# Quarters of a projection between table matmuls, a cumulative sum in halves inside the tile loop, and a plan moved behind a low part

## The chip, the cores and the metric

The kernel runs on one core of a Trainium2 chip. The metric is the device time of one execution in microseconds (us). PE is TensorE, DVE is VectorE, ACT is ScalarE, POOL is GpSimd, SP is SyncE.

## The reference

The input x has 2 x 1024 tokens of 256 columns. It is normalised per row (xn). Two branches are added to x:

- **Attention branch (a minGRU in log space).** k = xn W_z^T + b_z and y = xn W_h^T + b_h. Then `log_coeffs = -softplus(k)`, `log_values = -softplus(-k) + g(y)`, where g is log(relu(y) + 0.5) for y >= 0 and -softplus(-y) otherwise. a_star is the cumulative sum of `log_coeffs` **over the 256 columns** of each token, padded by a zero row; `log_h = a_star + cumlogsumexp(log_values - a_star)` along the tokens, with an initial value from h0. log_h is normalised by its global mean and deviation, exponentiated, added to xn and normalised per row with a weight and a bias.
- **Expert branch.** A router takes the softmax of xn w_gate^T, the top 2 of 8 experts per token, with weights that sum to 1. Each expert computes silu(x w1^T) * (x w3^T), then w2^T, with 704 hidden columns, scaled by the token's weight and summed.

## The kernel before

All token data lie transposed (256 columns as two groups of 128 partitions, 2048 tokens along the row) in four chunks of 512 tokens, c = 0 to 3. U holds the growing log values, A the growing softplus sums. Chunks 0 and 1 are the first batch, 2 and 3 the second.

**Front.** PE transposes xn, computes router logits and the projections: `project(c, mat, parts)` (L1183) has four matmuls, mat 0 for k and mat 1 for y. ACT reads them (`k_part`, L511, two activations; `k_log`, L517, abs, exp, log; `h_part`, L524, four activations). DVE works out which token goes to which slot of which tile of 128 rows (each expert has whole tiles, some 35 tiles in all). Eight groups of one-hot matmuls (the tables, L1256 to L1263, m = 0 to 7) turn that into index tables; DVE makes the one-hot matrix of each group (L896) in one of two buffers, so it may not be more than two ahead. After the last group DVE reads the table (L902 to L910): the gather index lets POOL start the row gathers (`gather(j)`, L384, four ahead), which PE transposes (`x_tile`, L1265), ACT rounds to a high part (`x_hi`) and DVE completes with a low part (`x_lo`).

**Cumulative sum.** It runs over the columns, that is over partitions: a triangular matrix times A for the first group, ones plus triangle for the second. `cumsum(c)` (L1201) does both groups of a chunk, six instructions of 512 columns, into two PSUM banks; DVE adds the result to U and to A (`add_cumsum`, L948). `half_cumsum(c, q)` (L1211) does one group into one bank, `add_half` (L957) adds it. Before, chunks 0 and 1 use the whole form ahead of the tile loop, chunks 2 and 3 the half form in tiles 4 to 7.

**Tile loop.** Tile j: PE runs `up(j)` (18 instructions of two column parts and a rest, L1301), the transposes of x for tile j+1, hooks (`between(j)`), `down(j-1)` (L1319), then `h_tile(j)` (L1331), the transposes of the gated rows, which need DVE's `gate(j)` (L976), which needs ACT's `silu(j)` (L608). ACT copies hT as a high part (`h_hi`, L603, for tile 0 L625), DVE makes its low part (`h_lo`, L971). DVE's own hooks `between(j)` and `after(j)` hold the attention work: add_l3, less_n, less_l2, run_max and so on, each a step on 1024 columns of a chunk or a group.

**Weights.** The next expert's weights are split in four pieces into high (ACT, L617) and low (POOL, L425) parts while the current expert's tiles run. `tile_experts` (L857) and `tile_plan` (L880) on DVE compute from the routing how many pieces are due by each tile; ACT and POOL read `plan` and wait for it (s_ctl) before their first pieces. SP reloads a piece's raw buffer when POOL is done with it (L339).

The order of all this is written out by hand, per engine; nothing plans it.

Of the kernel before, what the change touches and what calls it, by code (L numbers as in the profile page):

```python
# [39 lines left out]
CH = 512  # L40
# [12 lines left out]
def build_program(nc, x, small, w_main, w_tail, out, xn_dram):  # L53
# [5 lines left out]
    with ctx:  # L59
# [14 lines left out]
        A = sb("A", [P, 2 * NTOK])  # L74
# [26 lines left out]
        where, start = {}, 0  # L101
# [375 lines left out]
        def _(act):  # L477
# [33 lines left out]
            def k_part(c):  # L511
                act.wait_ge(s_kp, c + 1)
                for q in range(Q):
                    act.activation(chunk_of(U, c)[:, q, :], k_ps[:, q * CH:(q + 1) * CH], ACT.Identity,
                                   bias=bias_sb[:, 0, q:q + 1]).then_inc(s_kb, 1)

            def k_log(c):  # L517
                l1 = chunk_of(A, c)
                act.wait_ge(s_kb, 2 * c + 2)
                chain(act.activation(l1, chunk_of(U, c), ACT.Abs))  # L520
                chain(act.activation(l1, l1, ACT.Exp, scale=-1.0))
                act.activation(l1, l1, ACT.Ln, bias=1.0).then_inc(s_l1, 1)

            def h_part(c):  # L524
                act.wait_ge(s_k, c + 1)
                for sign, dst, b in ((1.0, chunk_of(xnT_M, c), bias_sb[:, 1, :]), (-1.0, nns[c], nbias[:, :])):
                    for q in range(Q):
                        act.activation(dst[:, q, :], yh_ps[:, q * CH:(q + 1) * CH], ACT.Relu,  # L528
                                       scale=sign, bias=b[:, q:q + 1]).then_inc(s_yr, 1)
# [11 lines left out]
            def h_log1p(c):  # L541
                act.wait_ge(s_ex, c + 1)
                act.activation(l2s[c], l2s[c], ACT.Ln, bias=1.0).then_inc(s_l2, 1)
# [29 lines left out]
            def x_hi(j, slot, src=xT_ps):  # L573
                act.wait_ge(s_xt, j + 1)
                act.activation(xT[:, slot, 0, :].rearrange("p (q n) -> p q n", q=Q), src, ACT.Copy).then_inc(s_xhi, 1)  # L575
# [9 lines left out]
            for c in range(2):  # L585
                h_log(c)
                h_exp(c)
                h_log1p(c)
            k_log(2)
            k_part(3)  # L590
            k_log(3)
            x_hi(0, 0, xT0_ps)
            x_hi(1, 1, xT1_ps)
            act.wait_ge(s_idx, 1)
            row_weight(0)
            row_weight(1)
            h_part(3)
            act.preload_act_table_set("silu_and_others")

            def h_hi(j):  # L600
# [16 lines left out]
                        act.activation(wslot(p // PIECES + 1, 0, part), raw[:, ds(part, WP)], ACT.Copy).then_inc(s_hi, 1)  # L617
                return done

            act.wait_ge(s_uc[0], 2)  # L620
            act.wait_ge(s_uc[1], 1)
            silu(0)
            act.wait_ge(s_ctl, 1)
            act.wait_ge(s_ht, 1)
            act.activation(hT[:, 0, :], hT_ps, ACT.Copy).then_inc(s_hhi, 1)  # L625
            split_due(0, 0)

            def y_copy(j):
# [115 lines left out]
        def _(dve):  # L744
# [203 lines left out]
            def add_cumsum(c):  # L948
                dve.wait_ge(s_cum, c + 1)
                u_wait(c)  # L950
                u_step(c, dve.tensor_tensor(chunk_of(U, c), chunk_of(U, c), grid(cum_ps), ALU.add))
                ins = dve.tensor_tensor(chunk_of(A, c), chunk_of(A, c), grid(cum_ps), ALU.add)
                a_step(c, ins)
                dve.wait_ge(s_ac[c], 1)
                dve.sem_inc(s_E, 1)

            def add_half(c, q):  # L957
                n = 2 * (c - 2) + (1 - q)
                dve.wait_ge(s_cumh, n + 1)
                u_wait(c)  # L960
                u_step(c, dve.tensor_tensor(chunk_of(U, c)[:, q, :], chunk_of(U, c)[:, q, :], cumh_ps, ALU.add))
                a_step(c, dve.tensor_tensor(chunk_of(A, c)[:, q, :], chunk_of(A, c)[:, q, :], cumh_ps, ALU.add))
# [115 lines left out]
            softplus(0)  # L1078
            softplus(1)
            tile_experts()  # L1080
            add_cumsum(0)
            less_l2(0)
            less_l2(1)
            x_lo(0, 0, xT0_ps)
            softplus(2)
            add_cumsum(1)
            x_lo(1, 1, xT1_ps)
            dve.wait_ge(s_u0b, 2)
            step(dve.tensor_tensor(u0t[:, 5, :], u0t[:, 3, :], u0t[:, 4, :], ALU.subtract))
            for b in range(B):  # L1090
                step(dve.tensor_tensor(u0[:, :].rearrange("p (q b) -> p q b", b=B)[:, :, b], u0t[:, 5, :],
                                       u0t[:, 0, :], ALU.add))
            gate(0)
            tile_plan()
            h_lo(0)
            add_l3(0)
            softplus(3)

            def between(j):
                if j == 1:  # L1100
                    less_n(0)
                if j == 2:
                    less_n(2)
                if j in (4, 5, 6, 7):
                    add_half(j // 2, 1 - j % 2)
                if j == 3:
                    run_max(0)
                if j in (8, 9):
                    run_max(j - 6)
                if j in (10, 12):  # L1110
                    run_scan(j - 10)
                if 13 <= j <= 16:
                    plus_max(j - 13)
                if 20 <= j <= 27:
                    row_stats(j - 20)

            def after(j):
                if j == 1:
                    add_l3(1)
                    less_n(1)  # L1120
                if j == 2:
                    less_n(3)
                if j == 3:
                    max_steps(0)
                    less_max(0)
                if j == 4:
                    run_max(1)
                if j == 5:
                    max_steps(1)
                    less_max(1)  # L1130
                if j == 6:
                    add_l3(2)
                    add_l3(3)
                if j == 7:
                    less_l2(2)
                    less_l2(3)
                if j in (8, 9):
                    max_steps(j - 6)
                    less_max(j - 6)
                if j in (11, 12):  # L1140
                    run_scan(1 if j == 11 else 3)
                if 13 <= j <= 16:
                    logh(j - 13)
                    if j < 16:
                        log_stats(j - 13)
                    else:
                        sums()
                if j == 17:
                    squares()
                if j == 18:  # L1150
                    normaliser()
                if j in (24, 28):
                    row_scales((j - 24) // 4)
                if 24 <= j <= 31:
                    last_norm(j - 24)
# [20 lines left out]
        def _(pe):  # L1176
# [21 lines left out]
                if n == 3:  # L1198
                    ins.then_inc(s_k if mat else s_kp, 1)

            def cumsum(c):  # L1201

                pe.wait_ge(s_c, c + 1)
                if c:
                    pe.wait_ge(s_E, c)
                pe.matmul(cum_ps[:, 0:CH], tri[:, :], chunk_of(A, c)[:, 0, :], start=True, stop=True)
                pe.matmul(cum_ps[:, CH:2 * CH], ones[:, :], chunk_of(A, c)[:, 0, :], start=True, stop=False)
                pe.matmul(cum_ps[:, CH:2 * CH], tri[:, :], chunk_of(A, c)[:, 1, :], start=False,
                          stop=True).then_inc(s_cum, 1)

            def half_cumsum(c, q):  # L1211

                n = 2 * (c - 2) + (1 - q)
                pe.wait_ge(s_c, c + 1)
                if n:
                    pe.wait_ge(s_ac[(n - 1) // 2 + 2], (n - 1) % 2 + 1)
                if q:
                    pe.matmul(cumh_ps, ones[:, :], chunk_of(A, c)[:, 0, :], start=True, stop=False)
                pe.matmul(cumh_ps, tri[:, :], chunk_of(A, c)[:, q, :], start=(q == 0), stop=True).then_inc(s_cumh, 1)
# [38 lines left out]
            for m in range(2 * NT // 4):  # L1258
                pe.wait_ge(s_pos, m + 1)
                for s in range(4):  # L1260
                    r = 4 * m + s
                    ins = pe.matmul(table_ps, onehot_pos[:, m % 2, s * P:(s + 1) * P],
                                    onehot_tile[:, r * NCOL:(r + 1) * NCOL], start=(r == 0), stop=(r == 2 * NT - 1))  # L1263
                ins.then_inc(s_posu, 1)

            def x_tile(j, k, val, dst=xT_ps):

# [1 line left out]
                for q in range(Q):  # L1269
                    ins = pe.transpose(dst[:, q, :], xg[:, k, q * P:(q + 1) * P], ident[:, :])  # L1270
                ins.then_inc(s_xt, 1)
            project(3, 0)
            cumsum(0)
            project(3, 1)
            x_tile(0, 0, 16, xT0_ps)
            x_tile(1, 1, 16, xT1_ps)
            cumsum(1)

            def either(e, products):

# [52 lines left out]

            pe.wait_ge(s_kb, 2 * NCH)
            up(0, 0, 0, lambda: pe.wait_ge(s_yr, 4 * NCH))
            pe.wait_ge(s_E, 2)
            h_tile(0)
            pe.wait_ge(s_eid, 1)

# [20 lines left out]
                ins.then_inc(s_htr, 1)  # L1360

            def between(j):
                if j in (4, 5, 6, 7):
                    half_cumsum(j // 2, 1 - j % 2)
                if 20 <= j <= 27:
                    h_back(j - 20)
# [69 lines left out]
```

## Time and profile before

| | us |
|---|---|
| median of three runs | 352.63 (350.98 to 352.78) |
| the profiled execution | 352.66 |
| its span | 350.8 |
| PE busy | 323.4 (92%) |
| DVE busy | 243.4 (69%) |
| ACT busy | 229.2 (65%) |
| POOL busy | 204.4 (58%) |

The shares are means over the whole span. The stretch that the change touches lies between 42 and 110 us: the tables, the first tile, and tiles 1 to 4. A group of rows below is read as: start, duration, engine, line, operation, and in brackets how long the engine was idle before it and what ended that. "Issue" is time in which the engine waited for nothing that the profile shows.

### The profile page before, as it was taken

The page shows a single profiled execution, that of the slowest core. Times are in us where ns is not written, and L with a number is a line of the kernel's source. Part 1 is how long each engine was busy: PE and PEld are TensorE (multiplying, and loading weights), DVE is VectorE, ACT ScalarE, POOL GpSimd, SP SyncE. Part 2 cuts the span into 40 slices and gives each one's busy share as a digit, 9 for nine tenths or more (in the row PEclk, how much of TensorE's full clock was granted, in tenths as well). Part 3 has the DMA queues.
Part 4 walks back from the last instruction along what each step waited for, and adds up shares of the span by engine and source line. Part 5 has one row for each costly group of instructions (what it writes and reads, how often), then busy time and mean ns, then how long its engine had stood idle before and what let it go on. Part 6 is the DMA issues. An engine that isn't in the chain of part 4 may idle for free.

```text
span 350.8 us, 6683 instructions
## 1 busy us (share of the span) xinstructions
PE 323.4 (92%) x1964; PEld 272.7 (78%) x1964; DVE 243.4 (69%) x430; ACT 229.2 (65%) x365; POOL 204.4 (58%) x137
## 2 busy tenths in 40 slices
PE   8998999898999999899989899999999999999950
PEld 8773474587878889788878788789998997999940
DVE  5488778989996779959889942455498767553410
ACT  2548898564889993899974349963955565443420
POOL 4600004249977763897789927765398458863531
PEclk9999969999999999999999999999999999999995
DMA  7952922005434642345346432544265265456431
GB/s 258 347 215 94 308 87 60 17 0 160 101 98 92 167 97 48 76 101 141 58 87 164 98 56 41 142 105 101 33 157 139 61 77 92 50 90 84 56 49 15
DMA packets 19087, 37.01 MB, mean 105 GB/s; under 512 B 2272, under 2 KB 13536, under 8 KB 19008
## 3 DMA queue, kind: packets, MB, share of 16 engines
q0 software_dynamic: 9168, 11.97, 21.7%
q1 hardware_dynamic: 8496, 22.56, 20.7%
q10 hardware_dynamic: 1376, 1.85, 1.5%
q8 instruction: 29, 0.48, 0.6%
q14 instruction: 18, 0.15, 0.1%
HBM read 27.45 MB, written 11.03 MB: 110 GB/s over the span
## 4 chain that ended last, share of the span: by engine, by line
PE 28%; issue 17%; ACT 15%; DVE 15%; DMA 13%; POOL 6%; POOLq 2%; ACTq 2%; DVEq 0%
PE PS L1301 9%; DMA out<-work,sidx 7%; PE PS L1195 7%; DMA out<-xrow 5%; PE PS L1319 4%; ACT L718 3%; POOL work L390 2%; PE PS L1331 2%; POOL out L406 2%; DVE tmp L976 2%; ACT tmp L608 2%; ACT L710 2%; ACT wbuf L617 2%; DVE hT L971 2%; DVE A L1013 1%
## 5 line engine op out<-in xcount | busy, mean ns | idle before, releaser
L1301 PE MATMUL PS<-wbuf,xT 128*128 128x512 f32 (+1 forms) x648 | 148.0, 382 | 4.4 <-issue 3.5
L1301 PEld LDWEIGHTS PS<-wbuf,xT 128*128 128x128 f32 x648 | 117.2, 188 | 28.3 <-issue 8.7
L425 POOL TENSOR_TENSOR wbuf<-raw,wbuf x28 | 78.7, 2822 | 27.4 <-ACT wbuf L617 26.6
L406 POOL DMA_INDIRECT out<-work,sidx x35 | 62.2, 1778 | 46.9 <-ACT work L634 24.8
L1319 PE MATMUL PS<-wbuf,hT 128*128 128x256 f32 x648 | 86.8, 288 | 0.0
L1319 PEld LDWEIGHTS PS<-wbuf,hT 128*128 128x128 f32 x648 | 79.3, 189 | 1.9 <-issue 1.9
L390 POOL DMA_INDIRECT work<-xn_dram,gidx x39 | 51.2, 1312 | 50.2 <-DVE gidx L907 36.8
L971 DVE TENSOR_TENSOR hT<-PS,hT 128x768 fp32r<-128x768 f32 x36 | 34.2, 950 | 46.1 <-ACT hT L603 45.1
L608 ACT ACTIVATE tmp<-PS 128x512 f32<-128x512 f32 x72 | 31.6, 459 | 38.8 <-PE PS L1301 38.7
L976 DVE TENSOR_TENSOR tmp<-tmp,PS 128x512 f32<-128x512 f32 x72 | 34.9, 515 | 28.8 <-ACT tmp L608 27.9
L1331 PE MATMUL PS<-ident,tmp 128*128 128x128 f32 x216 | 30.2, 276 | 6.1 <-DVE tmp L976 6.0
L634 ACT ACTIVATE work<-PS,wrow 128x256 f32<-128x256 f32 x35 | 16.4, 469 | 29.3 <-PE PS L1319 29.3
L603 ACT ACTIVATE hT<-PS 128x768 fp32r<-128x768 f32 x35 | 28.3, 810 | 10.5 <-PE PS L1331 10.5
L617 ACT ACTIVATE wbuf<-raw x28 | 30.4, 1110 | 4.7 <-issue 4.6
L1195 PE MATMUL PS<-xnT_M,small_sb 128*128 128x512 f32 x64 | 31.0, 624 | 1.7 <-ACT tmp L528 1.0
L1331 PEld LDWEIGHTS PS<-ident,tmp 128*128 128x128 f32 x216 | 23.9, 141 | 8.7 <-DVE tmp L976 7.7
L1195 PEld LDWEIGHTS PS<-xnT_M,small_sb 128*128 128x128 f32 x64 | 12.1, 202 | 14.0 <-issue 12.8
L710 ACT ACT_TABLE_LOAD x14 | 18.0, 1283 | 0.3
L718 ACT ACT_TABLE_LOAD x14 | 18.0, 1283 | 0.2
L967 DVE TENSOR_TENSOR xT<-PS,xT 128x256 fp32r<-128x256 f32 x37 | 15.5, 418 | 0.1
L575 ACT ACTIVATE xT<-PS 128x256 fp32r<-128x256 f32 x37 | 14.0, 382 | 1.6 <-PE PS L1270 1.6
L581 ACT ACTIVATE wrow<-work,first_pick 128x1 f32<-128x1 f32 x37 | 14.1, 385 | 0.0
(186 smaller groups left out, 367.3 us busy)
## 6 DMA issues: line engine op xcount, KB each, us to landing
raw<-w_main SPq DMA_DIRECT2D x24, 544.0 KB, 4.0
raw<-w_main SPq DMA_DIRECT2D x8, 416.0 KB, 3.5
xn_dram<-xrow SPq DMA_DIRECT2D x4, 516.0 KB, 5.9
out<-xrow POOLq DMA_DIRECT2D x4, 512.0 KB, 6.5
xrow<-x ACTq DMA_DIRECT2D x4, 256.0 KB, 5.8
xrow<-x SPq DMA_DIRECT2D x4, 256.0 KB, 5.2
small_sb<-small ACTq DMA_DIRECT2D x1, 768.0 KB, 8.3
work<-xn_dram,gidx POOLq DMA_INDIRECT x39, 4.1
```

The costliest lines, as they stand in the source:

```text
L390: pool.indirect_dma_start(xg[:, k, :], None, xn_dram, bass.IndirectOffsetOnAxis(gidx[:, j:j + 1], 0)).then_inc(s_gt[k], 16)
L406: pool.indirect_dma_start(out, bass.IndirectOffsetOnAxis(sidx[:, j:j + 1], 0), ysb[:, j % DEEP, :], None, compute_op=ALU.add).then_inc(s_s ...
L425: pool.tensor_tensor(lo, raw[:, ds(part, WP)], hi.bitcast(fp32), ALU.subtract).then_inc(s_w, 1)
L608: act.activation(sls[n], w1_ps[n], ACT.Silu).then_inc(s_silu, 1)
L617: act.activation(wslot(p // PIECES + 1, 0, part), raw[:, ds(part, WP)], ACT.Copy).then_inc(s_hi, 1)
L718: act.preload_act_table_set("silu_and_others")
L971: dve.tensor_tensor(hT[:, 1, :], hT_ps, hT[:, 0, :].bitcast(fp32), ALU.subtract).then_inc(s_hlo, 1)
L976: dve.tensor_tensor(g_hs[n], sls[n], w3_ps[n], ALU.mult).then_inc(s_g, 1)
L1195: ins = pe.matmul(PS[:, base + qo * CH:base + (qo + 1) * CH], wzh_sb[:, q, mat, qo * P:(qo + 1) * P], xnT[:, q, c * CH:(c + 1) * CH], star ...
L1301: ins = pe.matmul(PS[:, at:at + cols], xT[:, slot, xpart, q * P:(q + 1) * P], wbuf[:, w, wpart, q * 2 * F + at:q * 2 * F + at + cols], sta ...
L1319: ins = pe.matmul(y_ps, hT[:, hpart, c * P:(c + 1) * P], wbuf[:, w, wpart, W13 + c * D:W13 + (c + 1) * D], start=(c == 0 and hpart == 0 an ...
L1331: ins = pe.transpose(hT_ps[:, c * P:(c + 1) * P], g_h[:, a:a + P], ident[:, :])
```

## The change

PE: the four matmuls of `project(3, 0)` stand one each behind the table groups m = 3, 4, 5, 6, instead of all four behind the last group. `cumsum` is left for chunk 0 only, behind `project(3, 1)`. Chunk 1's sum becomes two half sums in the PE hook of tiles 1 and 2, and the waits of the half form count from chunk 1.

ACT: `k_part(3)` ahead of `k_log(2)`, `h_part(3)` ahead of the two x_hi, `k_log(3)` behind them. The wait for the plan moves behind the copy of hT in tile 0.

DVE: less_l2 and both x_lo ahead of `add_cumsum(0)`; `add_cumsum(1)` goes, `add_half(1, 1)` and `add_half(1, 0)` come into the hooks of tiles 1 and 2; `h_lo(0)` ahead of `tile_plan()`; add_l3 and less_n of chunks 0 to 3 change places within tiles 0 to 2.

```diff
@@ ACT @@
+            k_part(3)
             k_log(2)
-            k_part(3)
-            k_log(3)
+            h_part(3)
             x_hi(0, 0, xT0_ps)
             x_hi(1, 1, xT1_ps)
+            k_log(3)
             act.wait_ge(s_idx, 1)
             row_weight(0)
             row_weight(1)
-            h_part(3)
...
-            act.wait_ge(s_uc[0], 2)
+            act.wait_ge(s_uc[0], 1)
             act.wait_ge(s_uc[1], 1)
             silu(0)
-            act.wait_ge(s_ctl, 1)
             act.wait_ge(s_ht, 1)
             act.activation(hT[:, 0, :], hT_ps, ACT.Copy).then_inc(s_hhi, 1)
+            act.wait_ge(s_ctl, 1)
             split_due(0, 0)
@@ DVE @@
             tile_experts()
-            add_cumsum(0)
             less_l2(0)
             less_l2(1)
             x_lo(0, 0, xT0_ps)
+            x_lo(1, 1, xT1_ps)
+            add_cumsum(0)
             softplus(2)
-            add_cumsum(1)
-            x_lo(1, 1, xT1_ps)
...
             gate(0)
+            h_lo(0)
             tile_plan()
-            h_lo(0)
-            add_l3(0)
             softplus(3)
             def between(j):
                 if j == 1:
-                    less_n(0)
+                    add_l3(0)
+                    add_half(1, 1)
                 if j == 2:
-                    less_n(2)
+                    less_n(1)
+                    add_half(1, 0)
...
             def after(j):
                 if j == 1:
+                    less_n(0)
+                    less_n(2)
+                if j == 2:
                     add_l3(1)
-                    less_n(1)
-                if j == 2:
                     less_n(3)
@@ PE @@
                 ins.then_inc(s_posu, 1)
+                if 3 <= m < 7:
+                    project(3, 0, (m - 3,))
...
-            project(3, 0)
-            cumsum(0)
             project(3, 1)
+            cumsum()
             x_tile(0, 0, 16, xT0_ps)
             x_tile(1, 1, 16, xT1_ps)
-            cumsum(1)
...
             up(0, 0, 0, lambda: pe.wait_ge(s_yr, 4 * NCH))
-            pe.wait_ge(s_E, 2)
+            pe.wait_ge(s_E, 1)
...
             def between(j):
+                if j in (1, 2):
+                    half_cumsum(1, 2 - j)
                 if j in (4, 5, 6, 7):
                     half_cumsum(j // 2, 1 - j % 2)
```

## Rows read from the trace of the kernel before

**Rows 1.** Windows around the tables: stretch, engines' busy time, granted clock (PEclk), DMA.

```profile
45.00:49.00 4.00, 3.82 (x20) 3.62 (x19) 2.68 (x4) 3.97 (x6) 0.00 (x0) 0.59 0.19 74
49.00:53.00 4.00, 4.00 (x8) 2.09 (x9) 3.10 (x11) 3.94 (x5) 1.13 (x1) 0.56 0.00 0
```

**Rows 2.** Chain that ended last, from the tables to tile 0: start, us, what.

```profile
45.85 3.74 PE PS L1262 x16
...
62.80 0.86 PE PS L1208 x2
...
68.10 0.84 PE PS L1331 x6
```

**Rows 3.** PE in order of time: tables, up(1), h_tile(1), h_tile(2), h_tile(3).

```profile
44.44 1.23 PE L1262 MATMUL PS<-hT,xT 128*128 128x44 f32 x8 [0.34 <-DVE xT L896]
...
70.02 4.11 PE L1301 MATMUL PS<-wbuf,xT 128*128 128x512 f32 x18 [1.07 <-issue]
...
76.31 0.84 PE L1331 MATMUL PS<-ident,tmp 128*128 128x128 f32 x6
...
84.54 0.88 PE L1331 MATMUL PS<-ident,tmp 128*128 128x128 f32 x6 [0.58 <-DVE tmp L976]
85.72 4.10 PE L1301 MATMUL PS<-wbuf,xT 128*128 128x512 f32 x18 [0.30 <-issue]
...
92.01 0.82 PE L1331 MATMUL PS<-ident,tmp 128*128 128x128 f32 x6
```

**Rows 4.** DVE in order of time, from the first sum to gate(3).

```profile
57.30 1.22 DVE L951 TENSOR_TENSOR U<-U,PS 128x1024 f32<-128x1024 f32 x1 [0.33 <-PE PS L1208]
...
59.90 2.36 DVE L946 TENSOR_TENSOR U<-U,tmp 128x1024 f32<-128x1024 f32 x2 [0.24 <-DVE A L952]
62.17 0.42 DVE L967 TENSOR_TENSOR xT<-PS,xT 128x256 fp32r<-128x256 f32 x1
...
67.27 0.99 DVE L976 TENSOR_TENSOR tmp<-tmp,PS 128x512 f32<-128x512 f32 x2 [0.19 <-ACT tmp L608]
68.17 1.11 DVE L883 TENSOR_TENSOR wbuf<-hst,iota_c 128x924 fp32r<-128x924 f32 x1
...
75.53 0.95 DVE L976 TENSOR_TENSOR tmp<-tmp,PS 128x512 f32<-128x512 f32 x2
...
90.98 0.94 DVE L976 TENSOR_TENSOR tmp<-tmp,PS 128x512 f32<-128x512 f32 x2
```

**Rows 5.** ACT in order of time: table load, hT copy of tile 0, first weight pieces.

```profile
56.07 1.06 ACT L520 ACTIVATE A<-U 128x1024 f32<-128x1024 f32 x1
...
64.43 1.28 ACT L598 ACT_TABLE_LOAD   x1
...
71.44 0.81 ACT L625 ACTIVATE hT<-PS 128x768 fp32r<-128x768 f32 x1 [3.58 <-DVE plan L890]
72.90 2.12 ACT L617 ACTIVATE wbuf<-raw  x2 [0.64 <-issue]
```

**Rows 6.** The second gather on POOL, and time to landing of the first four.

```profile
54.15 1.05 POOL L390 DMA_INDIRECT work<-xn_dram,gidx  x1 [0.30 <-issue]
...
work<-xn_dram,gidx POOLq DMA_INDIRECT x4, 2.9
```

**Rows 7.** DVE and POOL side by side in tiles 1 to 4.

```profile
78.97 0.94 DVE L971 TENSOR_TENSOR hT<-PS,hT 128x768 fp32r<-128x768 f32 x1
...
84.83 3.13 POOL L425 TENSOR_TENSOR wbuf<-raw,wbuf  x1
85.00 4.05 DVE L941 TENSOR_TENSOR U<-U,tmp 128x1024 f32<-128x1024 f32 x1
...
101.57 0.67 DVE L961 TENSOR_TENSOR U<-U,PS 128x512 f32<-128x512 f32 x1
```

**Rows 8.** A later window, and POOL's scatter where it waits for ACT.

```profile
110.00:118.00 8.00, 8.00 (x45) 6.47 (x45) 5.72 (x10) 7.94 (x12) 7.19 (x4) 1.00 0.65 174
...
279.43 1.59 POOL L406 DMA_INDIRECT out<-work,sidx  x1 [4.92 <-ACT work L634]
```

More of the change, by code:

```diff
@@ L957, in add_half @@
             def add_half(c, q):
-                n = 2 * (c - 2) + (1 - q)
+                n = 2 * (c - 1) + (1 - q)
                 dve.wait_ge(s_cumh, n + 1)
@@ L1199, in project, with cumsum @@
                     ins.then_inc(s_k if mat else s_kp, 1)
[L1201 to L1208, printed above, removed]
+            def cumsum():
+                pe.wait_ge(s_c, 1)
+                pe.matmul(cum_ps[:, 0:CH], tri[:, :], chunk_of(A, 0)[:, 0, :], start=True, stop=True)
+                pe.matmul(cum_ps[:, CH:2 * CH], ones[:, :], chunk_of(A, 0)[:, 0, :], start=True, stop=False)
+                pe.matmul(cum_ps[:, CH:2 * CH], tri[:, :], chunk_of(A, 0)[:, 1, :], start=False,
                           stop=True).then_inc(s_cum, 1)
             def half_cumsum(c, q):
-                n = 2 * (c - 2) + (1 - q)
+                n = 2 * (c - 1) + (1 - q)
                 pe.wait_ge(s_c, c + 1)
                 if n:
-                    pe.wait_ge(s_ac[(n - 1) // 2 + 2], (n - 1) % 2 + 1)
+                    pe.wait_ge(s_ac[(n - 1) // 2 + 1], (n - 1) % 2 + 1)
                 if q:
```

## The prediction

> **What bounds the kernel now.** Times are us from the span's start; T is the end of the eight table matmul groups. I read four views in this order. First the granted clock by windows around the tables [rows 1]: the mean is 0.59 of full speed in 45 to 49 and 0.56 in 49 to 53. There are two levels, 1.00 (2.4 GHz) and 0.50 (1.2 GHz), and no other stretch near is low, so the clock was at half for 0.82 x 4 = 3.3 us of the first window and 0.88 x 4 = 3.5 of the second: it fell at about 45.7 and rose at about 52.5. The reader is to see that TensorE had been in the small table matmuls when it fell (group m = 3 of them ends at 45.67 [rows 3]) and was 3 us into the projection's long matmuls when it rose. 6.8 us at half speed cost 3.4 us of TensorE's work. Second the chain of waits [rows 2]: from the tables (T = 45.85 + 3.74 = 49.59) to up(0) at 63.66 it stands on PE and PE never idles. Third VectorE's rows [rows 4]: from T to gate(0) at 67.27, 17.68 us, it idles 0.33, 0.24 and 0.19 only. So two engines are full side by side in this stretch, and a gain on one is worth only what the other gives up. Fourth, ScalarE's wait for the plan (3.58) and its weight pieces after it [rows 5], the stretch from gate(1) to gate(3) [rows 3, 4], and what passes a delay on to the end [rows 8].
>
> **Part 1, quarters between tables.** The four quarters cost nothing more on PE, but they stand ahead of tables 4 to 7, and the gather index and all of VectorE's list start from the last table. From 45.67 there are 3.44 us of projection (eight instructions in four pairs; a pair of this width took 0.86 at full clock [rows 2]) and four tables; these ran without a gap at half clock, 3.74 us [rows 2], so 1.87 at full. Full clock all through: T = 45.67 + 3.44 + 1.87 = 50.98. If the clock falls at 45.7 as before, how long? It rose 2.9 us after projections began at 49.59; they now begin at 45.67, so I take it back by 49.1: 3.4 us at half clock, costing 1.7. T = 52.7. If it stays low as long as before, 3.4 lost, T = 54.4. Value taken: 52.7, with 51.0 and 54.4 as ends. The wait for the bias read of chunk 2 is long over. Project(3,1) then ends at T + 3.4 and cumsum(0) at T + 6.0 (3 times 0.86 [rows 2]); the sum of chunk 1 (2.58) is gone from here. PE would be free at T + 6.0.
>
> **Part 2, VectorE's list up to gate(0).** x_lo(0) began 12.58 behind T [rows 4]. Ahead of it now goes add_cumsum(0) (57.30 to 59.65, 2.35) with the idle 0.33 and 0.24: 9.66, and 0.4 for itself, so up(0) can start at T + 10.1 = 62.8, not at T + 6. gate(0) began 17.68 behind T; one add_cumsum (2.35) and the idle 0.76 leave: T + 14.6 = 67.3. h_tile(0) ended 1.68 after gate(0) began (67.27 to 68.94 [rows 2, 4]); now at 69.0. Before: 68.94. Difference 0.0, taken as 0. The ends follow T: -1.7 and +1.7. ScalarE is not later: gather(1) was issued 4.56 after T and lands 2.9 later [rows 6], x_hi(1) at about T + 8, then abs, exp and log (about 3.3 with the waits by its 1024-column rows of 1.06), row weights 0.7, table load 1.28 [rows 5]: silu(0) at T + 13.4 to 14, ahead of gate(0).
>
> **Part 3, plan behind h_lo(0), and the half sum in tile 1.** Before, h_tile(1) ended 8.21 after h_tile(0) (77.15 - 68.94 [rows 2, 3]). The plan took 68.17 to 71.41 (3.2), ScalarE waited for it, and its two pieces began 1.5 after it, of which the hT copy was 0.8 [rows 4, 5]. Now, counted from the end of h_tile(0): hT copy 0.85, h_lo 0.9 [rows 7], plan 3.2: 4.95. Pieces from 5.7 to 7.8, silu(1) behind them, gate(1) from about 8.45 to 9.3, h_tile(1) to 10.1. PE meanwhile has 1.07 of issue, up(1) 4.11, transposes 0.22, the new half sum with ones and tri 1.73, down(0) 2.14: 9.3, so it waits little. Cost 10.1 - 8.2 = +1.9. Bounds: PE alone adds 1.73 less its 0.34 of idle, +1.4; the whole plan on the path, +3.1. The two pieces end later by about as much, and with them POOL's low parts, gather(5) behind them and SP's reloads; POOL's queue then holds scatter(0), which nobody waits for until the copy of tile 4.
>
> **Part 4, tile 2.** One half sum of 0.86 on PE takes the place of 0.58 + 0.30 of idle [rows 3]; +0.1 (ends 0 and 2.0, the latter if gate(2) comes late as VectorE holds two more 1024-column steps before it).
>
> **Part 5, tile 3.** VectorE ran from gate(1) at 75.53 to gate(3) at 90.98, 15.45 us, without idle. It gets add_l3(0) 1.15 and four half steps (0.6 to 0.67 each, 2.5 [rows 7]): 19.1. In it three steps stood behind POOL's pieces; one took 4.05 against 1.22 beside a POOL step of 3.13 [rows 7]. With the half steps, which read PSUM, beside POOL instead, I count about 2.2 less blocked: 16.9. gate(1) begins 1.9 later, so gate(3) at 94.3, and h_tile(3) 95.7 to 96, against 92.83: +3.0 in all, +1.0 of it here. Ends 0 and 2.5.
> The Trainium skill, SBUF — State Buffer, section on practical consequences, says that a VectorE instruction with two SBUF inputs and a GpSimd instruction that reads SBUF block each other for the whole of the one that came first, while one with a single SBUF input does not contend. The trace agrees: h_lo (one PSUM input) took 0.94 in the middle of a POOL step, less_n 4.05. By that rule the moved halves are free of it and add_l3(0) is not, as above; if contention slowed all alike, the halves would double and part 5 would be near its upper end.
>
> **Sum.** 0 + 1.9 + 0.1 + 1.0 = +3.0 at the end of h_tile(3). Behind it PE is full (8.00 of 8.00 at 110 to 118) and POOL meets the pipeline again at 279.43, where it waited 4.92 for ScalarE's output copy [rows 8]; so a delay goes to the end one to one. Late stalls on VectorE belong to tiles, not to the clock on the wall, and move along. The profiled execution took 352.66 around a span of 350.8; the median shown is 352.63, the same. 352.66 + 3.0 = 355.7. I round down to 355.4, since T has its likelier error on the early side.
>
> **The rivals.**
> (a) PE is the bound and the rest follows: the 3.4 us lost at half clock come back in part or whole, and the rest adjusts: -1.7 to -3.4, so 349.3 to 351.0. For it: PE's unbroken rows from 45.85 to 66.5 and 92% busy. Against it: VectorE's list from T is as unbroken, and T moves late by 1.4 at least. It decides if x_lo(0) comes at T + 6 and the plan is no wait in tile 1. Chance 0.20. This is the other side.
> (b) The clock does not fall at all, as projection work comes in between: T = 51.0, sum +1.3, 353.9. For: the fall came just at the point where the first quarter will stand. Against: everything ahead of that point is unchanged. Chance 0.20.
> (c) PE idles from T + 6.0 to T + 10.1 but for four transposes; the clock, which fell after 2.4 us of small matmuls, falls again and up(0) runs at half. up(0) is 4.1 at full; gate(0)'s second half comes 1 to 1.2 later. Or the first low stretch stays as long as before (+1.7). 356.4 to 358.1, 357.1 taken. Chance 0.20.
> The Trainium skill, TensorE: Matmul & The Clock Gate, in Part 1 warns that idle gaps between bursts let the clock fall to half, and then the next burst starts cold. By this rule (c) would be likelier than I have it; no row here shows a plain idle gap of that kind, since the one fall stood in small matmuls.
> (d) My forecast, chance 0.40, own range 354.0 to 356.9.
>
> **How the numbers follow.** A measurement of this kernel can tell about 0.5%, 1.76 us, from no change: faster is under 350.9, slower over 354.4. (a) lies under it but for 0.03: 0.17, with 0.03 from other luck: 0.20. Same: (b) 0.14, (d) 0.07, (a) 0.03: 0.24. Slower: the rest, 0.56. The range leaves out about half of (a) and the end of (c): 350.0 to 358.0.
>
> **What would show it.** Part 1: last table group ends at 51 to 54.4, and the window 46 to 49 is at 0.50, 49.5 to 52.5 at 1.00. Part 2: PE idle of 3 to 4 us before up(0), x_lo(0) at T + 9.7. Part 3: ScalarE's pieces start 1.5 to 2.5 later, VectorE idle ahead of gate(1). Part 5: PE waiting on gate(3), h_tile(3) ending near 95.8, against 92.83. Wrong if h_tile(3) ends by 92.8, or if it ends late and a later stall shrinks.

## The result, and the profile after

The changed kernel takes 361.44 us (median of 6 runs, 360.5 to 362.59) against 352.26 us of the kernel before (median of 6): ratio 1.0265, 95% interval 1.0241 to 1.0290. It is slower by some 9 us. The forecast had the sign, not the size: 355.4 with a range up to 358.0. Times here and below are medians of all executions, while a ratio leaves out those over 1.5% above the fastest of their kernel, so the two can differ by some tenths of a per cent. The profiled execution of the changed kernel took 360.62 around a span of 358.8, so between the two profiles there are 8.0 us to find.

The page of the changed kernel, its busy times and its clock in 40 slices:

```profile
span 358.8 us, 6685 instructions
PE 326.4 (91%) x1964; PEld 275.8 (77%) x1964; DVE 241.0 (67%) x432; ACT 229.0 (64%) x365; POOL 203.9 (57%) x137
PEclk9999999899879999999999999999999999999986
```

VectorE's busy time is even less than before (243.4), and PE has the same 1964 instructions, with 3.0 us more of busy time (323.4 before). So the loss is waiting and clock, not work. PE in order of time (start, duration, line, operation, idle before and what ended it), the rows that answer to [rows 2, 3]; line numbers are one lower than before:

```profile
50.15 0.92 PE L1261 MATMUL PS<-hT,xT 128*128 128x44 f32 x4
...
61.29 5.63 PE L1300 MATMUL PS<-wbuf,xT 128*128 128x512 f32 x18 [2.30 <-issue]
67.52 0.85 PE L1330 MATMUL PS<-ident,tmp 128*128 128x128 f32 x6 [0.61 <-DVE tmp L976]
69.62 4.11 PE L1300 MATMUL PS<-wbuf,xT 128*128 128x512 f32 x18 [1.25 <-issue]
...
79.37 4.12 PE L1300 MATMUL PS<-wbuf,xT 128*128 128x512 f32 x18 [0.29 <-POOL wbuf L425]
...
87.11 4.10 PE L1300 MATMUL PS<-wbuf,xT 128*128 128x512 f32 x18
...
98.36 1.54 PE L1330 MATMUL PS<-ident,tmp 128*128 128x128 f32 x6 [4.80 <-DVE tmp L976]
99.55 5.75 PE L1300 MATMUL PS<-wbuf,xT 128*128 128x512 f32 x18
...
109.78 4.09 PE L1300 MATMUL PS<-wbuf,xT 128*128 128x512 f32 x18
```

The reader is to put the start of each up(j) beside that of before (up(1), up(3) from [rows 3]; up(2), up(4), up(5) began at 77.49, 92.91 and 102.13 there):

| up(j) starts | before | after | behind by | gained or lost in tile | forecast |
|---|---|---|---|---|---|
| j = 1 | 70.02 | 69.62 | -0.40 | | 0.0 |
| j = 2 | 77.49 | 79.37 | 1.88 | tile 1: +2.3 | +1.9 |
| j = 3 | 85.72 | 87.11 | 1.39 | tile 2: -0.5 | +0.1 |
| j = 4 | 92.91 | 99.55 | 6.64 | tile 3: +5.3 | +1.0 |
| j = 5 | 102.13 | 109.78 | 7.65 | tile 4: +1.0 | 0 |
| end | 352.66 | 360.62 | 8.0 | the rest: +0.3 | 0 |

Tile 3 is the surprise. VectorE and POOL from gate(1) to gate(3), the rows that answer to [rows 4, 7]:

```profile
77.46 0.95 DVE L976 TENSOR_TENSOR tmp<-tmp,PS 128x512 f32<-128x512 f32 x2 [2.85 <-ACT tmp L608]
78.67 1.58 DVE L936 TENSOR_TENSOR U<-U,xnT_M 128x1024 f32<-128x1024 f32 x1
...
82.23 2.64 DVE L941 TENSOR_TENSOR U<-U,tmp 128x1024 f32<-128x1024 f32 x2
...
85.95 3.12 POOL L425 TENSOR_TENSOR wbuf<-raw,wbuf  x1
85.99 4.18 DVE L941 TENSOR_TENSOR U<-U,tmp 128x1024 f32<-128x1024 f32 x1
...
90.30 0.69 DVE L961 TENSOR_TENSOR U<-U,PS 128x512 f32<-128x512 f32 x1
90.90 0.68 DVE L962 TENSOR_TENSOR A<-A,PS 128x512 f32<-128x512 f32 x1
91.50 0.95 DVE L971 TENSOR_TENSOR hT<-PS,hT 128x768 fp32r<-128x768 f32 x1
92.37 4.20 DVE L936 TENSOR_TENSOR U<-U,xnT_M 128x1024 f32<-128x1024 f32 x1
92.41 3.06 POOL L425 TENSOR_TENSOR wbuf<-raw,wbuf  x1
96.49 1.21 DVE L941 TENSOR_TENSOR U<-U,tmp 128x1024 f32<-128x1024 f32 x1
97.63 0.94 DVE L976 TENSOR_TENSOR tmp<-tmp,PS 128x512 f32<-128x512 f32 x2
```

Two steps of 1.21 us take 4.18 and 4.20: each began within 0.04 us of a POOL step and ended about 1.1 us behind it. Both stand ahead of gate(3) (97.63), though silu(3) was done at 91.58. Before, three steps of this stretch were stretched by POOL's pieces: two of them, shown here, and the one at 85.00 in [rows 7]. The second long one was run_max(0), 5.09 us at 92.17, which stood behind gate(3) (90.98):

```profile
76.73 2.32 DVE L941 TENSOR_TENSOR U<-U,tmp 128x1024 f32<-128x1024 f32 x1
...
79.83 2.69 DVE L936 TENSOR_TENSOR U<-U,xnT_M 128x1024 f32<-128x1024 f32 x1
...
91.99 3.12 POOL L425 TENSOR_TENSOR wbuf<-raw,wbuf  x1
92.17 5.09 DVE L983 TENSOR_TENSOR_SCAN xnT_M<-U,u 128x1024 f32<-128x1024 f32 x1
```

In the changed kernel PE then waits 4.80 us for gate(3), and the granted clock falls. Windows (stretch, busy times, granted clock behind POOL's):

```profile
92.00:98.30 6.30, 1.56 (x14) 1.36 (x12) 6.30 (x5) 2.83 (x4) 5.83 (x4) 0.85 0.56 132
98.30:102.00 3.70, 3.64 (x12) 3.16 (x13) 3.70 (x7) 2.05 (x3) 3.35 (x2) 0.50 0.53 93
102.00:106.00 4.00, 4.00 (x18) 3.24 (x17) 3.33 (x7) 2.25 (x5) 0.00 (x0) 0.85 0.13 33
```

PE had ended its work at 93.57 and stood idle until 98.36; a mean of 0.85 over 92.00 to 98.30 puts the fall to 0.50 (1.2 GHz) at about 96.4. h_tile(3) took 1.54 instead of 0.82 and up(4) 5.75 instead of 4.10. The same happened in up(0), 5.63 us, after the idle 2.30.

### The profile page after: what moved, and what is told of

The parts are those of the page before. It is cut to its first block, busy times and chain, and to the rows that moved or that the text cites. A ratio compares the mean times of both kernels' runs of the same rounds, so it can differ in the third digit from the quotient of the medians.

```text
span 358.8 us, 6685 instructions
## 1 busy us (share of the span) xinstructions
PE 326.4 (91%) x1964; PEld 275.8 (77%) x1964; DVE 241.0 (67%) x432; ACT 229.0 (64%) x365; POOL 203.9 (57%) x137
## 4 chain that ended last, share of the span: by engine, by line
PE 54%; DVE 16%; ACT 10%; issue 9%; DMA 4%; POOL 3%; ACTq 2%; POOLq 0%; DVEq 0%; SPq 0%
PE PS L1300 23%; PE PS L1318 12%; PE PS L1196 5%; PE PS L1330 5%; PE PS L1182 3%; DVE tmp L976 2%; DVE hT L971 2%; DMA out<-work,sidx 2%; DVE xrow L1074 2%; DVE U L941 2%; DVE U L936 2%; ACT L718 1%; DVE A L1013 1%; PE PS L1224 1%; ACT wbuf L617 1%
## 5 line engine op out<-in xcount | busy, mean ns | idle before, releaser
L1300 PE MATMUL PS<-wbuf,xT 128*128 128x512 f32 (+1 forms) x648 | 150.9, 387 | 6.4 <-issue 5.2
L1300 PEld LDWEIGHTS PS<-wbuf,xT 128*128 128x128 f32 x648 | 119.6, 192 | 30.5 <-issue 9.9
L425 POOL TENSOR_TENSOR wbuf<-raw,wbuf x28 | 80.8, 2895 | 26.9 <-ACT wbuf L617 25.7
L406 POOL DMA_INDIRECT out<-work,sidx x35 | 62.6, 1790 | 54.4 <-ACT work L634 33.2
L1318 PE MATMUL PS<-wbuf,hT 128*128 128x256 f32 x648 | 88.9, 292 | 0.0
L1318 PEld LDWEIGHTS PS<-wbuf,hT 128*128 128x128 f32 x648 | 81.0, 192 | 2.9 <-issue 2.9
L390 POOL DMA_INDIRECT work<-xn_dram,gidx x39 | 48.6, 1247 | 51.0 <-DVE gidx L907 38.0
L1196 PEld LDWEIGHTS PS<-xnT_M,small_sb 128*128 128x128 f32 x64 | 11.1, 190 | 10.4 <-issue 9.1
L1271 PE MATMUL PS<-ident,work 128*128 128x128 f32 x74 | 14.2, 273 | 0.9 <-DMA work<-xn_dram,gidx 0.9
```

The source lines that it names most:

```text
L390: pool.indirect_dma_start(xg[:, k, :], None, xn_dram, bass.IndirectOffsetOnAxis(gidx[:, j:j + 1], 0)).then_inc(s_gt[k], 16)
L406: pool.indirect_dma_start(out, bass.IndirectOffsetOnAxis(sidx[:, j:j + 1], 0), ysb[:, j % DEEP, :], None, compute_op=ALU.add).then_inc(s_s ...
L425: pool.tensor_tensor(lo, raw[:, ds(part, WP)], hi.bitcast(fp32), ALU.subtract).then_inc(s_w, 1)
L1196: ins = pe.matmul(PS[:, base + qo * CH:base + (qo + 1) * CH], wzh_sb[:, q, mat, qo * P:(qo + 1) * P], xnT[:, q, c * CH:(c + 1) * CH], star ...
L1300: ins = pe.matmul(PS[:, at:at + cols], xT[:, slot, xpart, q * P:(q + 1) * P], wbuf[:, w, wpart, q * 2 * F + at:q * 2 * F + at + cols], sta ...
L1318: ins = pe.matmul(y_ps, hT[:, hpart, c * P:(c + 1) * P], wbuf[:, w, wpart, W13 + c * D:W13 + (c + 1) * D], start=(c == 0 and hpart == 0 an ...
```

## The experiments

Ratios are to the kernel before on the same chip, with their 95% interval. "The lock" is the mutual blocking of VectorE and GpSimd (POOL) steps that part 5 of the prediction describes. Three theories stood at the start: A, the blocked VectorE steps ahead of gate(3) and the half clock behind them; B, the late plan and the late weight pieces; C, the front and the half clock in up(0).

**e1_plan_back**: in the changed kernel the plan and its wait as before.

```diff
@@ ACT @@
             silu(0)
+            act.wait_ge(s_ctl, 1)
             act.wait_ge(s_ht, 1)
             act.activation(hT[:, 0, :], hT_ps, ACT.Copy).then_inc(s_hhi, 1)
-            act.wait_ge(s_ctl, 1)
@@ DVE @@
             gate(0)
+            tile_plan()
             h_lo(0)
-            tile_plan()
```

> The changed kernel with one part undone: tile_plan() again ahead of h_lo(0) on VectorE, and ScalarE's wait for the plan again ahead of the hT copy of tile 0. Theory A (the time is lost where gate(3) comes 4.8 us late, because two VectorE steps of tile 2 each stand 3 us behind a POOL step, and in the half clock that follows): the pieces start about 2 us earlier and their places against VectorE's steps change, but tile 2 still holds both add_l3(1) and less_n(3) ahead of gate(3); 357 to 360. Theory B (the late plan and late pieces are the cause as a whole): 352 to 355. Theory C (the front and the half clock in up(0) are the cause): no change, 361.

Measured 360.11, ratio 1.0197 (1.0122 to 1.0273): 0.1 above A's range, far above B's, and not told apart from the changed kernel (1.0265). PE still waits 3.67 us for gate(3); the two blocked steps took 4.16 and 4.22. B as the whole cause falls.

**e2_late_steps**: add_l3(1) and less_n(3) behind gate(3), the first in the hook of tile 3, the second in that of tile 4.

```diff
                     add_half(j // 2, 1 - j % 2)
+                if j == 4:
+                    less_n(3)
                 if j == 3:
+                    add_l3(1)
                     run_max(0)
...
                     less_n(2)
-                if j == 2:
-                    add_l3(1)
-                    less_n(3)
                 if j == 3:
```

> The changed kernel with two VectorE steps moved from after(2), ahead of gate(3), to behind it: add_l3(1) just ahead of run_max(0), less_n(3) into tile 4. Same work, same front, same plan. Theory A: gate(3) comes at about 92.4 and not at 97.6, PE does not wait 4.8 us, the clock does not fall there; some of it comes back as run_max(0) and gate(4) are later: 354 to 358. Theories B and C: no change, 360.5 to 362.

Measured 357.93, ratio 1.0147 (1.0085 to 1.0209), within what A said. h_tile(3) no longer waits and the clock is 1.00 from 83 to 115; but gate(4) is late instead (0.98 us of PE wait), as run_max(0) now ends at 100.9. So 3.5 us of the 9 come back. The step on less_n(1), ahead of gate(3), is blocked here too (4.18 at 87.46).

**e3_no_quarters**: `project(3, 0)` whole behind the tables in the changed kernel.

> The changed kernel with project(3, 0) whole again behind the last table. Theory A: the tables end about 1.5 us earlier, VectorE's list to gate(0) with them, unless the clock falls in the tables again; tile 3 keeps its loss; 360 to 362. Theory C (the front is the cause): 353 to 357. If the quarters are what kept the clock up in the tables, the window 46 to 52 is at 0.50 again.

Measured 362.15, ratio 1.0271 (1.0219 to 1.0323), as A said to within 0.2. The clock was at 0.50 in 49 to 53 again, and PE waited 4.54 us for gate(3). Taking the quarters out does not mend the loss. That the quarters keep the clock up is not shown either: e1_plan_back has them, and its clock was at 0.50 in the same window.

**e4_warm**: a fill ahead of up(0) in the changed kernel.

```diff
@@ PE @@
             pe.wait_ge(s_kb, 2 * NCH)
+            for _ in range(30):
+                pe.matmul(PS[:, 0:P], ones_b[:, :], ones_b[:, :], start=True, stop=True)
             up(0, ...)
```

> The changed kernel with 30 bf16 matmuls of 128 columns on PE between the wait for the last bias read and up(0), where PE otherwise idles 2.3 us for x_lo(0). Theory C (PE's idle time lowered the clock in up(0), and that is carried to the end): up(0) takes 4.1 and not 5.6 us, 359 to 360. Theory A: at most 1 us, as gate(0) is held by ScalarE's silu only in part, and the 4.8 us wait of tile 3 remains: 360 to 361.5. If the fill has no effect on the clock, up(0) stays at 5.6.

Measured 360.08, ratio 1.0229 (1.0167 to 1.0290), not told apart from the changed kernel. The time lies where the ranges of A and C meet, so the trace has to decide. up(0) took 4.08, but up(1) took 5.66: in this execution the fall came one tile later, and the run did not take the half clock away. PE waited 4.69 us for gate(3). C as the main cause falls by the next run, in which up(0) is as slow as in the changed kernel (5.64) and most of the loss is gone.

**e6_swap**: the changed kernel with two neighbouring steps of tile 2 exchanged. It separates a lock from plain load, since the work is the same.

```diff
                 if j == 2:
-                    less_n(1)
                     add_half(1, 0)
+                    less_n(1)
```

> The changed kernel with two VectorE steps of tile 2 in the other order: add_half(1, 0), which reads PSUM, ahead of less_n(1), which reads two SBUF tiles. Same steps, same tile, same POOL work. Theory A1 (the lock: a step with two SBUF inputs that starts beside a POOL step waits for its whole 3.1 us, and the two engines stay in step from one blocking to the next): the half step fills 1.3 us of the first blocking, add_l3(1) then starts ahead of the next POOL step, gate(3) comes 3 to 4 us earlier, and the half clock behind it shrinks or goes: 356 to 358.5. Theory A2 (VectorE simply has too much work ahead of gate(3), whatever its order): 360.5 to 362.

Measured 354.64, ratio 1.0053 (1.0022 to 1.0083): about 7 us less than the changed kernel, from the order of two steps, and 1.4 under the range of A1, which had priced the gain too low. The two profiled executions have the same front (up(1) starts at 69.25 and 69.62); up(4) starts at 94.67 instead of 99.55, up(5) at 103.24 instead of 109.78, and the end is 7.6 us earlier (352.98 and 360.62). VectorE and POOL in e6_swap:

```profile
85.63 3.13 POOL L425 TENSOR_TENSOR wbuf<-raw,wbuf  x1
85.67 0.67 DVE L961 TENSOR_TENSOR U<-U,PS 128x512 f32<-128x512 f32 x1
86.27 0.67 DVE L962 TENSOR_TENSOR A<-A,PS 128x512 f32<-128x512 f32 x1
86.86 2.99 DVE L941 TENSOR_TENSOR U<-U,tmp 128x1024 f32<-128x1024 f32 x1
89.78 0.94 DVE L971 TENSOR_TENSOR hT<-PS,hT 128x768 fp32r<-128x768 f32 x1
90.65 1.21 DVE L936 TENSOR_TENSOR U<-U,xnT_M 128x1024 f32<-128x1024 f32 x1
91.78 1.21 DVE L941 TENSOR_TENSOR U<-U,tmp 128x1024 f32<-128x1024 f32 x1
92.80 3.09 POOL L425 TENSOR_TENSOR wbuf<-raw,wbuf  x1
92.92 0.94 DVE L976 TENSOR_TENSOR tmp<-tmp,PS 128x512 f32<-128x512 f32 x2
...
94.11 3.94 DVE L983 TENSOR_TENSOR_SCAN xnT_M<-U,u 128x1024 f32<-128x1024 f32 x1
```

The half steps run at their full pace inside the POOL step (0.67 each), and less_n waits for the rest of it only (2.99). The next POOL step finds gate(3), which reads PSUM, and not add_l3(1), which has run at its full pace (1.21 at 90.65). PE's wait for gate(3) is 0.44 and the clock stays at 1.00 there. Theory A2, load alone, falls.

**The parts one by one on the kernel before.** b1_plan_behind has the plan and its wait moved, nothing else; b2_halves the half sums of chunk 1 in tiles 1 and 2; b3_quarters the quarters, project(3, 1) ahead of cumsum(0) and ScalarE's order.

> The kernel before with one part of the change alone: tile_plan() behind h_lo(0) and ScalarE's wait for it behind the hT copy. By the prediction's third part tile 1 gets 0 to 2 us longer, as there is no half sum on PE to cover the later silu(1), and VectorE has room in tiles 2 and 3: 353 to 355. Theory B (the plan is the cause of the 9 us): 359 to 362.

Measured 354.28, ratio 1.0042 (1.0018 to 1.0067), as part 3 expected. up(2) started at 80.44, 2.95 later than before, with up(1) at half clock (5.65) and gate(1) waiting 1.71 us for ScalarE; 0.8 of it was back by up(4) at 95.09.

> The kernel before with one part alone: chunk 1's sum in two halves in tiles 1 and 2, in place of cumsum(1) and add_cumsum(1) ahead of the tiles. PE and VectorE have the same work in total; up(0) can start 1 to 2.6 us earlier, VectorE gets 2.5 us more ahead of gate(3). Theory A: gate(3) is late by 3 or more, 355 to 359. Theory B or C: 351 to 353.

Measured 357.42, ratio 1.0093 (1.0055 to 1.0131), which is A's range. Its ten executions fall into two groups, four at 353.5 to 355.0 and six at 357.3 to 359.5. The profile is of a long one (358.61) and has the loss of the changed kernel in small; what the short ones did differently no profile shows.

```profile
90.66 4.42 DVE L941 TENSOR_TENSOR U<-U,tmp 128x1024 f32<-128x1024 f32 x1
90.93 3.07 POOL L425 TENSOR_TENSOR wbuf<-raw,wbuf  x1
95.01 0.94 DVE L976 TENSOR_TENSOR tmp<-tmp,PS 128x512 f32<-128x512 f32 x2
...
95.74 1.54 PE L1331 MATMUL PS<-ident,tmp 128*128 128x128 f32 x6 [3.22 <-DVE tmp L976]
96.93 6.20 PE L1301 MATMUL PS<-wbuf,xT 128*128 128x512 f32 x18
```

> The kernel before with one part alone: the quarters of project(3, 0) between the tables, project(3, 1) ahead of cumsum(0), and ScalarE's order of the changed kernel. cumsum(1) stays ahead of up(0), so PE has no long idle time there. The last table 1.4 us later, or less where the clock stays up; VectorE's list follows. Theory A: 352 to 354. Theory C (the front is the cause): 357 or more.

Measured 355.20, ratio 1.0091 (1.0058 to 1.0124): 1.2 us above the upper end of A, under C. The executions spread from 353.5 to 357.9, and the profiled one (353.56) is nearly the shortest. In it up(1) starts at 71.63, 1.6 later than before; VectorE waited 0.68 us for cumsum(1), which began behind PE's wait of 2.04 us for add_cumsum(0) and ran at half clock.

**g1_halves_swap**: b2_halves with add_half(1, 0) ahead of less_n(2), the same mend on the other kernel.

> The kernel before with chunk 1's sum in halves (as in b2_halves), and in tile 2 add_half(1, 0) ahead of less_n(2). The same two steps in b2_halves stood the other way round. Lock theory: the half step (PSUM) runs beside the POOL step, less_n(2) waits for its rest only, less_n(3) ends ahead of the next POOL step, PE does not wait for gate(3) and the clock stays up: 352 to 354, 3 to 5 under b2_halves. Load theory: as b2_halves, 355 to 358.

Measured 352.58, ratio 1.0008 (0.9987 to 1.0030), the interval clear of that of b2_halves. One execution of twelve took 460.91, far outside the rest. The lock theory holds a second time: less_n(2) takes 2.86, less_n(3) ends at 91.3 ahead of the POOL step at 92.28, and PE does not wait.

**Mends together on the changed kernel**: e6_swap with the plan put back (g2), with the fill (g3), with both (g4).

> e6_swap (the changed kernel with the two steps of tile 2 swapped) with the plan again ahead of h_lo(0). By b1_plan_behind the plan behind h_lo(0) costs about 1.5 us: 351.5 to 354, if the pieces do not fall worse against VectorE's steps; by the lock theory they can, and then PE waits for gate(3) again, 355 or more.

> e6_swap with the 30 small matmuls ahead of up(0) that kept the clock up in e4_warm. up(0) 1.5 us shorter, part of it taken back as gate(0) waits for VectorE: 352.5 to 354.5; if the clock falls one tile later instead, as it did in e4_warm in up(1), no gain: 354 to 355.

> e6_swap with the plan ahead of h_lo(0) and the fill, all three mends together. If all that the runs so far showed adds up, this is the best of them: 350 to 353, a tie with the kernel before or just under it. If the front's later table is what is left, 353 to 355.

Measured: g2 352.80, ratio 1.0013 (0.9986 to 1.0040), in its first range; g3 354.82, 1.0067 (1.0030 to 1.0104), in its range for no gain; g4 352.91, 1.0016 (0.9993 to 1.0038), in its first range. With the swap and the plan put back the changed kernel is not told apart from the one before; how much of that is the plan stays loose, as the intervals of e6_swap and g2 overlap. The fill adds nothing on top. No version beat the kernel before.

The reason expected for g3, that the clock falls one tile later, is not what its profile shows. Both tiles ran at full clock:

```profile
65.53 4.09 PE L1300 MATMUL PS<-wbuf,xT 128*128 128x512 f32 x18 [0.71 <-DVE xT L967]
...
72.74 4.11 PE L1300 MATMUL PS<-wbuf,xT 128*128 128x512 f32 x18 [1.22 <-issue]
```

Yet this execution took 357.32. Its front was late: in the tables the clock was at 0.50 from about 46.3 to 56.5, and VectorE read the table at 55.30 instead of 50.76 in e6_swap.

**The front differs from one execution to the next.** This can be read by setting the 14 profiles side by side. In the five without quarters (before, e3, b1, b2, g1) the clock fell in the tables each time, and VectorE read the table at 48.7 to 49.6. In the nine with quarters it stayed at 1.00 in five (the changed kernel, e4, e6, b3, g4), and the table was read at 50.6 to 51.3. In the other four it fell, and the table was read at 52.57 (e2), 54.05 (e1), 55.35 (g2) and 55.30 (g3). Three of these four took longer than the median of their kernel (361.42, 355.29 and 357.32 against 360.11, 352.80 and 354.82). So moving the projection ahead of the last tables exposes the gather index to the clock. How often the clock falls there, and whether the quarters have a part in it, these single profiles cannot say.

## Why the prediction was wrong

**Part 5 is the step that failed**, in the sentence "With the half steps, which read PSUM, beside POOL instead, I count about 2.2 less blocked: 16.9". VectorE from gate(1) at 77.46 to gate(3) at 97.63 took 20.2 us. Before, the blocked time in this stretch was 1.1 + 1.5 + 2.8 = 5.4; I put down 3.2; measured are 0.4 (add_l3(0), 1.58), 0.3, 2.96 and 2.98, together 6.6. The difference of 3.4 is the whole miss of 3.3 in that stretch: gate(3) came at 97.63, forecast 94.3. In the profile 8.0 us were lost where 3.0 were forecast. Of these 5.0, 3.3 are this step, 1.3 the half clock behind it (0.3 up to the start of up(4), 1.0 in tile 4), and 0.3 came later. The lock and its price were right; what was missing is the time line. The prediction gave a count of blocked time and never said which VectorE step each POOL step would meet. Of the two long blockings, both fell ahead of gate(3) (on less_n(1) and add_l3(1)), where before one of them fell behind it, on run_max(0). A small shift in such a position is worth 3 us: in e6_swap less_n(1) begins 0.87 later than in the changed kernel (86.86 and 85.99), and add_l3(1) takes 1.21 instead of 4.20. My ends for this part, 0 and 2.5, had no such jump in them; tile 3 took 5.3 more.

The Trainium skill, SBUF — State Buffer, section Summary: rules for kernel authors, says of this pair that the second one to issue is blocked until the first has finished. The traces agree on the blocking, and on the order only in part. At 85.99 POOL's record began first (85.95). At 92.37 VectorE's did, by 0.04 us, and in b2_halves by 0.27 us (90.66 and 90.93), and still it was VectorE's step that was stretched (4.20 and 4.42) and POOL's that kept its 3.06 and 3.07. So in a time line a VectorE step that starts just ahead of a POOL step is to be priced as blocked too.

**The position was no accident of one run.** In the changed kernel, e1 and e2 the two engines meet at the same step: 85.99 and 85.95, 86.36 and 86.32, 87.46 and 87.43. Both are released together when the POOL piece ahead ends, POOL then has a gather and the start of a scatter, VectorE the rest of less_n, gate and x_lo, and these are of the same length. After the block the same again: 92.37 and 92.41 in the changed kernel, 92.72 and 92.76 in e1. The kernel before has such pairs as well, somewhat wider: 85.00 and 84.83, 92.17 and 91.99. That the common release is what aligns them is my reading of the rows; shown by the runs is that the pairs recur and that another order of two steps ends it. All six executions of the changed kernel took 360.5 or more. In b2_halves, whose times lie in two groups, it may have been less fixed.

**The clock behind it was left out.** I had idle time lower the clock in rival (c), ahead of up(0), and priced none for tile 3. It cost 0.7 in h_tile(3) and 1.65 in up(4). Tile 4 kept 1.0 of it, as other parts of the tile were shorter: from h_tile(4) to up(5) it took 0.57 (109.21 to 109.78), before 1.02 (101.11 to 102.13).

**What held.** Part 1: the last table group ended at 51.07, the early end of my range, as the clock stayed at 1.00 from 45 to 53; in e1 it was 0.70 and 0.50 over 45 to 49 and 49 to 53, and in e2 0.58 and 1.00, so that differs between executions. My late end, 54.4, was too low: in g2 and g3 the table was read at 55.3. Part 2: up(0) started at 61.29, T + 10.2 (forecast T + 10.1), gate(0) at 66.69, T + 15.6: 1 us more than forecast, as up(0) ran at half clock and silu(0) was late. That is the condition of rival (c), and it came true; its time did not. T was 1.6 early, so up(1) still started 0.40 ahead of before, and 361.44 lies beyond the 356.4 to 358.1 of (c). Part 3: +2.3 for +1.9; ScalarE's pieces began at 74.83, 1.9 later, and VectorE idled 2.85 ahead of gate(1); b1_plan_behind gives the plan alone 1.5 us of the whole time. Part 4: -0.5 for +0.1. Its reason for a late gate(2), two more 1024-column steps, was miscounted: there are three such steps from gate(1) to gate(2) before and after, and the half sum's two of 512 columns are what is added. Passed on one to one to the end: 7.65 at up(5), 8.0 at the end.

Rival (a), in which PE's recovered half clock time decides, is refuted: the changed kernel recovered it in full and was ready for up(0) early, and idled. Rival (b)'s clock came, its time did not.

What stays open: the parts alone add up to 1.0042, 1.0093 and 1.0091, together 2.3%, near the whole 2.65%, while one swap takes 2% away and the same swap in b2_halves takes 0.85%. So the parts' losses are not sums of independent terms, and how much of b3_quarters' 0.9% is the later table, how much the clock in the tables, which stayed up in its profile and may not in its longer executions, and how much cumsum(1)'s wait was not taken apart.

## What to carry to other kernels

When you move steps on an engine that shares a lock with another, lay the other engine's steps on the same time line and ask for each step which one it meets; price a step that reads two SBUF tiles with both outcomes, and put both in the range. Steps fed from PSUM are the ones to set beside a GpSimd step, and steps with two SBUF inputs belong behind the gate that TensorE waits for. A wait of some microseconds on TensorE can cost more than its length, since what ran next here ran at 1.2 GHz. And profile a kernel more than once before a reading rests on its front: the same front had its clock at either level.

## What the runs showed of the hardware

The lock is sharp: 4.18, 4.20, 4.16 and 4.22 us for steps of 1.21 us that began within 0.04 us of a POOL step of 3.06 to 3.12, whichever began first by the profile. Where VectorE's record began 0.27 us ahead (b2_halves), it was 4.42. PSUM-fed steps inside a POOL step took 0.67 or 0.68, the same as with no such step beside them (0.67 at 101.57 before).

The clock fell after short waits, but not each time. In the changed kernel 2.30 us of idle, behind two pairs of transposes with 0.87 between them, came ahead of a half clock up(0). With 30 small matmuls in that gap up(0) ran at full clock in all three profiles that have them, and up(1) took 5.66 (e4), 5.46 (g4) and 4.11 (g3). The kernel before ran up(1) at full clock (4.11) after 67 to 70, in which PE was busy for 1.35 of 3.00 us; b1_plan_behind, busy for 1.74 of 3.00 there, ran it at half clock (5.65).
